# A four-layer fused kernel on Trainium2: norms, transposes and projections at four seams between its stages put in another order

## What is computed

```python
x = _layernorm(x + _L0_attn_ref(x, Wq, Wk, Wv, Wo))      # 16 heads, rope, softmax
x = _layernorm(x + _L0_ffn_ref(x, W1, W2, W3))           # silu(x W1) * (x W3), Walsh-Hadamard, W2
x = _layernorm(x + _L1_attn_ref(x, ...))                 # mLSTM with 8 heads, then a gated MLP
x = _layernorm(x + _L1_ffn_ref(x, ...))                  # gated FFN with int8 weights
```

## Time and profile before

| | us |
|---|---|
| median of 3 runs | 680.57 (678.65 to 680.57) |
| the profiled execution | 680.19 |
| its span, first to last instruction | 678.2 |
| the second block starts (barrier) | 405.97 |
| last matmul | 670.51 |

### The profile page before, as it was taken

One profiled execution on the slowest core, in us unless ns is written; L12 is line 12 of the kernel. 1 busy time (PEld: TensorE's weight loads), 2 busy tenths in 40 slices (PEclk: granted clock), 3 DMA queues, 4 the chain that ended last, 5 costly groups with the idle time before them and its releaser, 6 DMA issues. The chain is left out here.

```text
span 678.2 us, 15318 instructions
## 1 busy us (share of the span) xinstructions
PE 660.3 (97%) x5290; PEld 635.7 (94%) x5290; DVE 441.7 (65%) x966; ACT 410.3 (60%) x1085; POOL 244.5 (36%) x275
## 2 busy tenths in 40 slices
PE   8999999999999999999999989999999999999995
PEld 8899999999999999999999979999887799999995
DVE  5656567557665765765675575656667986556776
ACT  5566677666776666766676853333679864334552
POOL 2731862134353223622338544112544350122101
PEclk8999999999999999999999999999999999999998
DMA  7174664436534445543364204100256100000000
GB/s 251 30 205 162 200 171 141 130 103 173 173 121 111 120 128 180 159 136 108 98 197 140 63 1 149 32 0 15 59 174 264 46 1 1 1 1 0 1 31 32
DMA packets 38156, 69.74 MB, mean 103 GB/s; under 512 B 3424, under 2 KB 22624, under 8 KB 37856
## 3 DMA queue, kind: packets, MB, share of 16 engines
q1 hardware_dynamic: 37680, 68.38, 33.2%
q10 hardware_dynamic: 432, 0.79, 0.4%
HBM read 52.18 MB, written 16.97 MB: 102 GB/s over the span
## 5 line engine op out<-in xcount | busy, mean ns | idle before, releaser
L312 PE MATMUL PJ<-xTh,WBh 128*128 128x256 f32 x364 | 106.7, 293 | 0.0
L314 PE MATMUL PJ<-xTh,WBl 128*128 128x256 f32 x364 | 102.8, 282 | 0.0
L313 PE MATMUL PJ<-xTl,WBh 128*128 128x256 f32 x364 | 102.8, 282 | 0.0
L830 POOL TENSOR_TENSOR stage<-stage 128x256 f32<-128x256 f32 x32 | 24.5, 765 | 165.1 <-DVE stage L692 165.1
L585 ACT ACTIVATE probs<-probs,rinv 128x256 f32<-128x256 f32 x128 | 58.4, 508 | 28.3 <-DVE rinv L708 28.3
L1208 PE MATMUL UG<-xTh,WBh 128*128 (+1 forms) x256 | 73.6, 288 | 1.0 <-PEq L54 1.0
L1211 PE MATMUL UG<-xTh,WBl 128*128 (+1 forms) x256 | 72.5, 283 | 0.0
L1209 PE MATMUL UG<-xTl,WBh 128*128 (+1 forms) x256 | 72.5, 283 | 0.0
L1265 ACT ACTIVATE ga<-UG 128x256 f32<-128x256 f32 x64 | 24.5, 382 | 76.3 <-PE UG L1211 76.2
L312 PEld LDWEIGHTS PJ<-xTh,WBh 128*128 128x128 f32 x364 | 69.2, 190 | 0.4
L313 PEld LDWEIGHTS PJ<-xTl,WBh 128*128 128x128 f32 x364 | 69.3, 190 | 0.0
(11 more groups left out here) (302 smaller groups left out, 2407.8 us busy)
## 6 DMA issues: line engine op xcount, KB each, us to landing
K<-scr_k SPq DMA_DIRECT2D x60, 256.0 KB, 4.5
raw<-in_w_att SPq DMA_DIRECT2D x37, 256.0 KB, 4.8
Q<-scr_q SPq DMA_DIRECT2D x15, 512.0 KB, 7.4
stage<-scr_m SPq DMA_DIRECT2D x6, 768.0 KB, 5.0
scr_q<-rot_h SPq DMA_DIRECT2D x30, 128.0 KB
scr_q<-rot_l SPq DMA_DIRECT2D x30, 128.0 KB
scr_k<-rot_h SPq DMA_DIRECT2D x30, 128.0 KB
scr_k<-rot_l SPq DMA_DIRECT2D x30, 128.0 KB
```

Source lines behind the costliest of these rows:

```text
L312: pe.matmul(out, ah, bh, start=(i == 0), stop=False)
L313: pe.matmul(out, ah, bl, start=False, stop=False)
L314: last = pe.matmul(out, al, bh, start=False, stop=(i == n - 1))
L830: pool.tensor_tensor(y[:, 0:S], c[:, 0:S], sn[:, S:2 * S], ALU.subtract).then_inc(rope_sum, 1)
```

## The change

- Attention's end: the transpose of batch 0, `tail(4)`, moves from after head 2 to after head 3 and that of batch 1 stays as `tail(5)`; `norm_apply(0)`, `norm_stats(1)` move one head later on DVE, and `norm_apply(1)` goes behind the loop. The third norm, `tail(6)` and `split_batch(2)` leave attention. Batch 2 is now normed in the first chunk of the first FFN: `dve_stats` at step 0, `dve_apply` at step 1, `pe_T` at step 2, `act_hi` and `dve_lo` at step 3.
- The last three `down` of every FFN (`last_down`) do the products with the high part first and wait for the low part only ahead of the last two matmuls. Before the very last one of the first FFN, PE projects batch 0's queries.
- The last transpose of the third FFN's input, `pe_T(3, 3)`, moves into the second chunk, which is now written out.
- mLSTM: all gates of batches 0 to 2 before `pe_T(1, 3)`, batch 3's right after it and batch 0's values; batch 3's queries, keys, values and output gates are projected inside the heads, into the banks `X` and `TB`. The orders of ACT and DVE follow. SP issues the last MLP weight piece after the first rows of `scr_m`. POOL starts the MLP pieces after batch 3's `xs`, and the second six after `chain`.

```diff
-        TAIL = [(0, 1), (2,), (3, 4), (5,)]
+        TAIL = [(0, 1), (2,), (3,), (4,)]
...
-            tail(6)
...
             pT(last_u, 3)
+            tail(4)
             oT(last_u - 1, 15, 2)
             tail(5)
             oT(last_u, 15, 3)
-            tail(6)
...
                         if j == 0:
                             norm_stats(0)
-                        if j == 1:
+                        if j == 2:
                             norm_apply(0)
                             norm_stats(1)
-                        if j == 2:
-                            split_batch(0)
-                            norm_apply(1)
                         if j == 3:
-                            norm_stats(2)
+                            accumulate(14, 14)
 
             dve.memset(mhalf[:, :], -0.5).then_inc(mh_set, 1)
...
             pT(last_u, 3)
+            norm_apply(1)
             oT(last_u - 1, 15, 2)
+            split_batch(0)
+            oT(last_u, 15, 3)
             split_batch(1)
-            norm_apply(2)
-            oT(last_u, 15, 3)
-            split_batch(2)
 
         @block.gpsimd
...
-            return FT - 1 if kind == 2 and k == BEFORE[2] else T_STEP[k]
+            return None if kind == 2 and k == BEFORE[2] else T_STEP[k]
...
+            def last_down(ht):
+
+                at = [slice(t * P, (t + 1) * P) for t in range(TT)]
+                pe.wait_ge(q["f_hi"], FT * (B - 1) + ht + 1)
+                for t in range(TT):
+                    pe.matmul(OUTS[:, t, 0:D], fh[:, ht, at[t]], w_down(kind, ht), start=False, stop=False)
+                    if kind != 2:
+                        pe.matmul(OUTS[:, t, 0:D], fh[:, ht, at[t]], w_down(kind, ht, False), start=False, stop=False)
+                pe.wait_ge(q["f_lo"], FT * (B - 1) + ht + 1)
+                for t in range(TT):
+                    last = pe.matmul(OUTS[:, t, 0:D], fl[:, ht, at[t]], w_down(kind, ht), start=False, stop=(ht == FT - 1))
+                last.then_inc(q["down"], 1)
...
+                if k == 0 and ht == 2:
+                    pe_T(pe, 0, B - 2)
...
-                down(B - 1, ht, False)
+                if fill and ht == FT - 1:
+
+                    pe.wait_ge(q["gated"], FT * B - 3)
+                    fill()
+                last_down(ht)
...
+            if k == 0 and ht == 0:
+                dve_stats(dve, 0, B - 2)
+            if k == 0 and ht == 1:
+                dve_apply(dve, 0, B - 2)
+            if k == 0 and ht == 3:
+                dve_lo(dve, 0, B - 2)
...
+        VOG_STEP = [(0, 2), (1, 1)]
+        V_STEP = [(0, 3), (1, 2)]
+        OG_STEP = [(1, 0), (1, 3)]
...
-            more(RING, 12)
+            more(RING, 11)
...
+            more(11, 12)
...
+            def qk_piece(c, i):
+
+                if c == B - 1:
+                    if i == 0:
+                        pe.wait_ge(s_["gcol_ready"], 1)
+                        pe.wait_ge(s_["enm_ready"], 1)
+                elif c:
+                    pe.wait_ge(s_["qk_split"], 2 * c - 1 + i)
+                for n in range(2):
+                    w = slice((2 * i + n) * P, (2 * i + n + 1) * P)
+                    last = six(qk_bank(c, i)[:, n * S:(n + 1) * S], [(WLh[:, t, w], WLl[:, t, w]) for t in range(KT)],
+                               x_parts(c))
+                last.then_inc(s_["qk_ready"], 1)
...
                 if c == 0:
+                    qk_piece(B - 1, 0)
                     scores(0, 0)
                     scores(0, 1)
+                    qk_piece(B - 1, 1)
...
+                    if (c, pair) in VOG_STEP:
+                        vog_piece(B - 1, VOG_STEP.index((c, pair)))
...
-            project(0)
-            for c in range(B - 2):
+            ffn_pe(pe, 0, fill=first_queries)
+            project_qk(0)
+            for c in range(B - 1):
                 project_gates(c)
             pe_T(pe, 1, B - 1)
-            project_gates(B - 2)
-            project_qk(1)
+            project_vog(0)
             project_gates(B - 1)
             project_vog(1)
-            project(2)
+            project_qk(1)
+            project_vog(2)
             rows_T()
-            project(3)
+            project_qk(2)
             for c in range(B):
                 heads(c)
 
...
+            def turn_last(ht):
+                if ht == 0:
+                    pe_T(pe, 3, 3)
+            ffn_pe(pe, 2, None, turn_last)
...
             mlp_hi(0, 5)
-            act_ssq(act, 1, 3)
             evac_q(0)
             evac_k(0)
+            act_ssq(act, 1, 3)
+            act_hi(act, 1, 3)
             evac_og(0)
-            act_hi(act, 1, 3)
             mlp_hi(5, 6)
+            gates()
+            mlp_hi(6, 7)
+            evac_og(1)
             evac_q(1)
-            mlp_hi(6, 7)
             evac_k(1)
-            gates()
             mlp_hi(7, 8)
-            evac_og(1)
+            evac_og(2)
             mlp_hi(8, 9)
+            exp_nm()
+            mlp_hi(9, 10)
             evac_q(2)
-            mlp_hi(9, 10)
             evac_k(2)
-            evac_og(2)
             mlp_hi(10, 11)
-            exp_nm()
+            decay(0, 0)
+            decay(0, 1)
             evac_q(3)
             mlp_hi(11, 12)
-            evac_k(3)
-            decay(0, 0)
-            decay(0, 1)
-            evac_og(3)
             decay(0, 2)
             decay(0, 3)
+            evac_k(3)
             for c in range(B):
                 for pair in range(PAIRS):
                     if pair:
...
                     for u in (HM * c + 2 * pair + 4, HM * c + 2 * pair + 5):
                         if u < HM * B:
                             decay(u // HM, u % HM)
+                    if (c, pair) in OG_STEP:
+                        og_tile(B - 1, OG_STEP.index((c, pair)))
                     if pair == 1 and c:
...
             dve_apply(dve, 1, 3)
+            split_qk(0)
             dve_xs(dve, 1, 3)
-            split(0)
             dve_lo(dve, 1, 3)
-            split(1)
+            take_values(0)
+            take_values(1)
             chain()
-            split(2)
+            split_qk(1)
+            take_values(2)
             dve.wait_ge(s_["rows_ready"], 1)
             dve.tensor_copy(gcol[:, :, :], X[:, 0:S].rearrange("p (t h) -> p t h", t=TT)).then_inc(s_["gcol_ready"], 1)
-            split_q(3)
+            split_q(2)
             mask_rows(0, 0)
-            split_k(3)
+            split_k(2)
             mask_rows(0, 1)
-            take_v(3, 0)
-            take_v(3, 1)
             for c in range(B):
                 for pair in range(PAIRS):
                     weigh(c, 2 * pair)
...
                     if c == 0 and pair == 0:
                         mask_rows(0, 2)
                         mask_rows(0, 3)
+                        split_qk(3)
+                    if (c, pair) in V_STEP:
+                        take_v(B - 1, V_STEP.index((c, pair)))
...
-            split_mlp(0, 12)
+            pool.wait_ge(s_["xs_ready"], N_RMS[1] + B)
+            split_mlp(0, 6)
+            pool.wait_ge(s_["nm_ready"], 1)
+            split_mlp(6, 12)
```

More of the change, by code:

```diff
@@ L495, in emit @@
                         values(u - 2, *back, (j - 2) % 4, first=(k == 0 and j == 2))
-                    if k == 15 and j < 3:
+                    if k == 15:
                         for q in TAIL[j]:
@@ L770, in emit @@
                         accumulate(13, 13)
-                    if k == 15 and j == 3:
-                        accumulate(14, 14)
                     if j == ROPE_STEP and k < 14:
@@ L915, in _ @@
             split_down(0)
-            for c in range(B - 1):
+            for c in range(B - 2):
                 pool.wait_ge(ln_aggr, TT * (c + 1))
@@ L926, in _ @@
                     split_down(3)
[L930 removed]
+N_LN = {0: 2 - B, 1: 2, 3: 2 + B, 4: 2 + 2 * B}
 N_RMS = {1: 0, 2: B}
[L932 removed]
+N_T = {0: 2 - B, 1: 2, 2: 2 + B, 3: 2 + 2 * B}
 N_ADD = {1: 0, 3: B, 4: 2 * B}
@@ L1193, in chunks, with ffn_pe @@
                 chunk(c, False)
-        def ffn_pe(pe, kind, first_hook=None, second_hook=None):
+        def ffn_pe(pe, kind, first_hook=None, second_hook=None, fill=None):
             q = ffn_sems[kind]
@@ L1279, in hook @@
             def hook(k, c, ht):
+                if k == 0 and ht == 3:
+                    act_hi(act, 0, B - 2)
                 if ht == 3 and k in N_RMS:
                     act_ssq(act, k, c)
-                if k in N_T and ht == min(t_step(kind, k) + 1, FT - 1):
+                if k in N_T and t_step(kind, k) is not None and ht == t_step(kind, k) + 1:
                     act_hi(act, k, c)
@@ new lines, in vog_piece, with first_queries @@
+            def vog_piece(c, t):
+                if c == B - 1:
+                    pe.wait_ge(s_["qk_split"], 2 * c + 1 + t)
+                elif c:
+                    pe.wait_ge(s_["og_ready"], 2 * (c - 1) + t + 1)
+                rows = slice(t * P, (t + 1) * P)
```

(30 more changed lines are left out.)

51 lines of the change are left out of this document (28 added, 23 removed).

## The result

| | before | after |
|---|---|---|
| median of the runs, us | 680.57 | 688.31 |
| lowest, highest, us | 678.65, 680.57 | 686.66, 690.33 |
| profiled execution, us | 680.19 | 689.45 |
| its span, us | 678.2 | 687.4 |
| ratio after to before | | 1.0125, 95% interval 1.008 to 1.0169 |

The change costs 1.25%; I had predicted 682.7 with a range up to 685.2. A second series on another chip gave 688.6 us and a ratio of 1.0108 (1.0048 to 1.0168). In part of the executions of the kernel before (17 of 28 in the longest series) the mean granted clock is 0.970 to 0.976 instead of 0.994 to 0.997 and the time 9 us or more longer; the ratios leave such executions out, except that one of 688.64 us slipped into those of the second series, which without it are 1.0136 here, 1.0088 for the filled wait in the heads and 0.9975 for the last experiment.

What follows compares the result with a forecast made beforehand. The prediction took PE's one long row of matmuls (busy 660.3 of 678.2 us) as the bound. Its terms, -1.4 + 4.55 + 1.4 - 0.8 - 1.25 = +2.5 us on 680.19, gave 682.7 us, range 679.3 to 685.2.

Steps and rivals of the forecast that it cites:

- Attention's end: End of attention: batch 0's norm wait goes and the next block starts earlier, though `tail(5)` waits longer; -1.4 us.
- Batch 2's norm: First FFN: PE waits at batch 2's transposes because `BN_AGGR` waits for the small load `sdown`; +4.55 us.
- the clock, +1.4: First FFN: behind the stall at batch 2's norm the granted clock falls to 0.50 for 3.40 us; +1.4 us.
- First FFN's end to the heads: Last `down` of the first FFN through the heads: waits removed and ACT's lead outweigh new waits; -0.8 us.
- Second and third FFN: `pe_T(3, 3)` no longer waits for its copy and the last `down` waits less; -1.25 us.
- The heads lose: Rival, heads: longer `weigh` waits because the last weight piece lands late; +1.5 instead of -0.8, 685.0 us; chance 0.15.
- The clock holds: Rival, first FFN: the clock doesn't fall through the stall at batch 2's norm; 681.3 us; chance 0.2.
- the norm is in time: Rival, first FFN: small loads land in time, PE waits only 1.15 us and the clock stays; 677.9 us; chance 0.08.
- the reorder of gates and heads pays in full: Rival, gates and heads: ACT's lead carries through, -2.7 instead of -0.8; 680.8 us; chance 0.17.

Runs made afterwards that it cites:

- the filled wait in the heads: Changed kernel with 20 unread matmuls put into PE's wait in front of the third pair of heads: 684.47 us, ratio 1.0088.
- the last experiment: The three edits and the step later, with batch 1's normalisation on DVE moved earlier in attention's end: 677.47 us, ratio 0.9975.
- The three edits: Changed kernel, batch 2's norm not waiting for small loads, last weight piece behind batch 3's keys (ACT), their split behind second `weigh` pair (DVE): 678.99 us, ratio 0.999.
- the piece behind keys: Changed kernel with the last weight piece on ACT behind two decays and batch 3's keys instead of ahead: 685.9 us, ratio 1.0092.
- the split behind `weigh`: Changed kernel with the split of batch 3's keys on DVE behind the second pair's `weigh` instead of ahead: 684.26 us, ratio 1.0071.
- the step later: The three edits, with batch 2's transposes, copy and split in the first FFN one step later: 677.29 us, ratio 0.9965.
- the norm freed: Changed kernel with batch 2's norm no longer waiting for the four small loads: 683.79 us, ratio 1.006.
- attention undone: Changed kernel with all of attention and batch 2's norm as before the change: 684.2 us, ratio 1.0069.
- stall filled: Changed kernel with 30 unread matmuls put into PE's stall in the first FFN: 687.2 us, ratio 1.0121.
- the old order in the heads: Changed kernel with gates, projections and heads as before, batch 2's norm not waiting for small loads: one execution 678.06 us, five 688.9 to 694.2.

## Why the prediction was wrong

- **Attention's end, -1.4 us: right.** The block starts at 404.76, 1.88 us earlier with the execution's own lag of 0.63 taken out (I had 1.8); `tail(5)` stood idle for 1.44 us behind `norm_apply(1)`, 1.61 in the prediction's count from start to start (I had 1.45), and 392.21's wait is gone.
- **Batch 2's norm, +4.55, and the clock, +1.4: right.** 4.34 us of idle time at the place (4.51 from start to start), with the releaser and through the chain I had named; the slow stretch was 3.4 us long, 1.7 us lost. The stretch is 6.55 us longer, against 4.55 + 1.4 and 0.4 of work that moved in. The row of `sdown` (5.4 us) was the price to take: it landed in 5.3. That it came so close was partly luck, since six profiled executions of this order have 4.0 to 5.4, and the stall goes with it. By the Trainium skill's page "DMA: Bandwidth & Descriptors" (anatomy of one DMA), 2.0 us and the bytes, the landing was estimated at 2.3; the page has that figure for a DMA that GpSimd issues, this one is SyncE's, and none of the traces agrees with it.
- **First FFN's end to the heads, -0.8: this step failed.** It measured +5.26. From start to start, the single waits were placed well up to the third one: `pe_T(1, 3)` 1.18 us (I had 1.1), the first scores 0.73 (0.75). Then the third `weigh` cost 2.88 us over the matmuls' pace, where I had 1.4 to 1.9. Its chain was the one I had named, but I counted ACT's two decays and the piece's copy, not ACT's 1.43 us of standing still until the piece had landed: I had written that mechanism down as a rival and priced it at half the waits again. That is some 1.2 of the 6 us by which the term was wrong.
- **The second fall of the clock, 3.4 us, was in no case of mine.** 6.8 us at half clock lose 3.4, and filling the wait gave back 3.5. I had priced this for a stall of 4.5 us and not asked it of one of 1.4 to 1.9, though the start of the program showed a fall behind 1.90 us of idle time.
- **The remaining 1.5 us were gains booked without a row, and a price left out.** The three edits, with a third wait of only 0.73 us and the full clock, are 0.2 us ahead of before; with the wait that I had placed (1.65) they would be 0.7 behind, where I had -0.8. Their trace and that of before show three things. I took 0.8 of PE's losses in the rest of the heads for ACT's lead, but up to the first `ho` transposes PE lost only 0.5 us there before, and it loses 0.3 instead now, in front of those transposes. Of the about 1 us of slow scores (eight score matmuls took 1.07 us instead of 0.61 at 509.31 and again at 511.44) only half went: behind the third wait they still take 1.07. And the moved projections cost more between the scores: six matmuls of 512 columns lengthen a pair of heads from 1.95 to 3.54 us, so by 1.59, where six of them took 1.38 in a row; twelve of 256 columns take 1.62 instead of 1.44. That is 0.6 us for moving work, which I had put at nothing. Together the three are about the 1.5 us.
- **Second and third FFN, -1.25: right.** -1.21 measured.
- **The rivals.** "The heads lose" came, at +5.26 instead of its +1.5. "The clock holds", "the norm is in time" and "the reorder of gates and heads pays in full" did not.

The right terms make 3.34 us of the 9.23 (-1.88 + 6.55 - 0.12 - 1.21), the failed one 5.26, and 0.63 is the execution's later start, which no edit touches.

## What to carry over

A stall has two prices where PE's clock can fall behind it: its own length and the slow stretch. Here the second was as large as the first in the heads, and the two together made most of the way from a term of -0.8 to +5.26; so ask of every wait that an edit leaves or moves whether the clock has fallen behind one of that length in this trace. When a step moves ahead of a point where a semaphore stands for several loads, look which of them it really needs: one condition on a shared wait was worth 4.5 us. And where one engine's queue has an item that waits for a transfer, what stands behind it on the next engine decides whether anyone notices: moving one split behind the urgent work took PE's wait from 2.68 to 0.54 us.

## What the runs showed of the hardware that I had not expected

- **The clock in the heads falls on little.** The granted clock fell to 0.50 behind 2.68, 1.18 and 0.54 us of idle time (the changed kernel, the piece behind keys, the split behind `weigh`). It stayed at 1.00 behind 0.53 and 0.65 us in the profiled executions of the three edits and the step later, and behind 1.15 us where 20 matmuls in a row followed. What separates 0.54 from 0.53 stays open: PE's starts in the heads up to there are the same to 0.02 us. A stall in the first FFN, 100 us earlier, doesn't decide it alone: the clock fell in the kernel with the norm freed, which has 1.18 us there, and held in the one with the filled wait, which has 3.13.
- **It stays low for very different times.** In the dense `up` matmuls of the first FFN it was low for 3.4 us in four executions and for 6.8 in a fifth; in the heads with batch 3's twelve-matmul projections among them for 3.4 us (split behind `weigh`), 6.8 (the changed kernel twice, attention undone, piece behind keys) and 10.2 (norm freed, stall filled); in the heads as they were before for 26.5 us, in the one execution traced. So the changed order may have a merit which the comparison leaves out, that the clock comes back sooner. Its means point that way: with the three edits, the step later and the apply earlier no execution of 30 is below 0.993, while the kernel before has 17 of 28 at 0.970 to 0.976, and the traced execution with the old order in the heads has 0.977. That the projections do this is not shown; no such execution of the kernel before was traced.
- **The landing of one 128 KB broadcast load** took 4.0 to 5.4 us in the thirteen profiled executions, with the same three loads issued in front of it.
- **DVE beside POOL:** the apply of 0.73 us took 2.06 when POOL's cast and subtraction ran beside it. The same is in the earlier trace rows: 1.25 us for the apply at 390.81, and `xs` 2.67 against 0.61.
